# Softmax attention of a two-layer tower on one Trainium2 core: one ordered stream through the score banks

## The chip, the cores and the metric

The kernel runs on one core of one Trainium2 chip. Its engines work side by side and meet only at semaphores: TensorE (PE: matmuls and transposes, results in the eight 2 KB-a-partition banks of PSUM), VectorE (DVE), ScalarE (ACT), GpSimd (POOL) and SyncE (SP, which here issues DMAs). The metric is device time of one execution in microseconds; lower is better.

## What is computed

A tower of two layers over 16 sequences of 1024 tokens with 64 channels. Layer 0: six token embeddings, a ternary linear layer, a linear attention, a mixture of experts. Layer 1: the softmax attention that this document is about, and a second feed-forward block with attention-like parts. Between them stand residual additions and layer normalizations.

```python
h = tok(x, itok...)                       # (16, 1024, 64)
h = h + L0_attn(layernorm(h));  h = h + L0_ffn(layernorm(h))
h = h + L1_attn(layernorm(h));  h = h + L1_ffn(layernorm(h))

def L1_attn(v, WQ, WK, WV, Wout, bout):   # 8 heads of 64 channels
    q, k, val = (v @ WQ), (v @ WK), (v @ WV)          # split in heads
    scores = einsum('bshc,bthc->bsth', q, k) * SCALE
    A = softmax(scores, axis=2)
    u = einsum('bsth,bthc->bshc', A, val).reshape(B, S, H * C)
    return u @ Wout + bout
```

## The kernel before

The stages run one after the other, with a barrier between them: layer 0 (to 1019 us), `attention1` (1020 to 3472 us), statistics and residual, `feedforward1`, `finish1`. Only `attention1` is touched.

**What a head does.** The weights of a head are folded, so that the scores are x_k . (Wa x_q): `wa` makes the query of a head from the batch's input, and `wvo` folds the value and output weights. Everything wants the input transposed: `a_xh` is its float16 value and `a_xl` the rest (high and low half of a float32), both 128 partitions x 1024: two copies of the 64 channels, one in partitions 0 to 63, one in 64 to 127. A query is held likewise as `a_qh` and `a_ql`, with the 1024 queries laid as two halves of 512 over the two groups of 64 partitions. So most products run as two matmuls side by side, one on each half of the array's rows ("64*128" in the profile's rows), or, where the result has 64 rows, one on each half of its columns ("128*64").

Channel 0 of the input is set to 1. Row 0 of each half of `a_qh` is overwritten with minus the largest score of each query: the score product then gives score minus maximum, ready for the exponential. That largest score must be known before the head starts, so it is found two heads and one head ahead from a coarser product, high half times high half.

**A step.** A head has eight steps, one for each tile of 128 keys. In step kt TensorE does in this order:
1. `score(x, kt + 1)` (L1343): six matmuls of 64 x 512 into banks 0 and 1, or 2 and 3 (two score pairs in turn);
2. the side tasks of the step (table `a_tasks`): nearly always one `max` (L1298), two matmuls into two of the three banks 4, 5, 7, which VectorE reduces to a maximum per query (L1415, L1417);
3. `values(x, kt)` (L1351): exponentials times input, float32, two matmuls of 64 x 512 added into bank 6 (`A_SUM`) over the eight steps.

ScalarE takes the exponential (L1270) of a score pair to `a_prob`, four buffers. After the exponential of step 0 it copies the former head's sums from bank 6 to `a_un` (L1257), and `values(x, 0)` waits for that copy (`s.copied`).

**Other side tasks.** They too take banks of the three, in one ring numbered by j, where a task waits until the occupant three places before was taken:
- step 1, `out` (L1330): the output product of the former head, two banks; VectorE takes reciprocals of the sums of exponentials (L1429) and scales (L1431), GpSimd adds to `h` (L1221);
- step 2, `q` (L1306): the query of the head after next, one bank; ScalarE writes `a_qh` (L1249), VectorE subtracts and writes `a_ql` (L1406);
- step 6, `row` (L1321): eight transposes of one column each turn the maxima `a_mm` into rows in one bank; VectorE copies the two halves into `a_qh` (L1422, L1423);
- in head 5 of a batch, steps 3 and 5, `x` (L1314): four transposes each of the next batch's input; ScalarE writes `a_xh`, VectorE `a_xl`.

A loop (`Fori`) covers 16 heads, two batches; it runs 8 times. Each engine has the unrolled 16 heads as its own program, in the order in which the code emits it; nothing is scheduled otherwise. `feedforward1` is built differently: there ScalarE reads one ordered stream through the four score banks, its banks 4, 5, 7 hold only maxima and a row, GpSimd splits into halves, and the row goes by SyncE's DMAs. It is unchanged, and its rows are used below.

## Time and profile before

| | us |
|---|---|
| median of 3 runs (6041.11 to 6046.69) | 6045.32 |
| the profiled execution | 6043.24 |
| its span, first to last instruction | 6041.5 |
| TensorE busy (share of the span) | 5173.9 (86%) |
| VectorE busy | 4295.8 (71%) |
| ScalarE busy | 3124.6 (52%) |
| GpSimd busy | 1654.3 (27%) |
| ScalarE, exponentials of the attention (L1270), 1024 of 1113 ns | 1139.8 |
| VectorE, its maxima (L1415, L1417), 2070 of some 685 ns | 1419.0 |

The profile is that of one execution. A busy share of the span is a mean over stages with different limits; what matters for a change in one stage are the rows of that stage. A matmul's end is modelled: matmuls overlap in the array, so distances are read from start to start. A row of the timeline has start, duration, engine, line, operation, result<-operands, the part of the array (rows*columns) and the shape, and xN for N merged instructions; in brackets stands how long the engine was idle before, and whose end ended that.

### The profile page before, as it was taken

Reading aid. Unit: us, or ns where it says so; the run is one execution under the profiler, and the core shown is the slowest. Engines: PE = TensorE matmul, PEld = TensorE weight load, DVE = VectorE, ACT = ScalarE, POOL = GpSimd, SP = SyncE. Lnnn points to the kernel's source line nnn. Section 1 sums busy time; section 2 is a strip of 40 time slices with the busy share of each in tenths; the row PEclk is TensorE's granted clock in tenths of the full one; section 3 lists DMA queues with packets and bytes.
Section 4 is the critical chain, followed back from the end, with each engine's and each line's share of the span. In section 5 each row is a group of like instructions: output and inputs, shape, how many; then the busy total and the mean of one; then the engine's idle time right before and its main releaser. Section 6 shows DMA issues by size and latency. Waiting matters only on the chain. (4 is left out here: it accounts for less than half of the span.)

```text
span 6041.5 us, 124050 instructions
## 1 busy us (share of the span) xinstructions
PE 5173.9 (86%) x43090; PEld 2166.3 (36%) x43120; DVE 4295.8 (71%) x7936; ACT 3124.6 (52%) x3244; POOL 1654.3 (27%) x1572
## 2 busy tenths in 40 slices
PE   2678777999999999999999959999999999998454
PEld 1344343222222222232223224444444444443222
DVE  2666665767676767676767658888888888887666
ACT  0222221555555555555555517777777777775111
POOL 1022213000010100000000146555565565554000
PEclk9788877999999999999999959999999999998555
DMA  1211110000000000000000000000000000000000
GB/s 31 66 42 42 42 42 0 1 2 1 2 1 2 1 2 1 2 1 2 1 2 1 1 1 2 3 2 3 3 2 3 3 2 3 2 3 2 10 7 10
DMA packets 41419, 52.58 MB, mean 9 GB/s; under 512 B 31060, under 2 KB 31191, under 8 KB 40792
## 3 DMA queue, kind: packets, MB, share of 16 engines
q1 hardware_dynamic: 37734, 43.54, 2.9%
q8 instruction: 367, 6.01, 0.4%
q14 instruction: 260, 2.13, 0.1%
q10 hardware_dynamic: 3058, 0.89, 0.1%
HBM read 39.68 MB, written 4.19 MB: 7 GB/s over the span
## 5 line engine op out<-in xcount | busy, mean ns | idle before, releaser
L2054 DVE TENSOR_REDUCE f_mp<-psum 128x1 f32<-128x512 f32 (+2 forms) x2614 | 1343.5, 574 | 236.7 <-PE psum L1902 183.4
L1270 ACT ACTIVATE a_prob<-psum,escale 128x1024 f32<-128x1024 f32 x1024 | 1139.8, 1113 | 612.8 <-PE psum L1343 605.1
L1852 ACT ACTIVATE f_prob<-psum,escale_f 128x1024 f32<-128x1024 f32 x1152 | 1242.8, 1112 | 280.5 <-PE psum L1970 150.0
L1351 PE MATMUL psum<-a_prob,a_v 128*64 128x512 f32 x4096 | 1101.0, 616 | 0.1
L1415 DVE TENSOR_REDUCE a_mp<-psum 128x1 f32<-128x512 f32 x1035 | 715.5, 691 | 516.0 <-PE psum L1298 496.9
L1221 POOL TENSOR_TENSOR h<-h,a_u 128x512 f32 x129 | 163.6, 1268 | 2203.8 <-DVE a_u L1431 2203.8
L1892 PE MATMUL psum<-f_kf,f_qf 64*128 64x512 f16 (+3 forms) x3138 | 680.3, 333 | 52.0 <-DVE f_mp L2054 44.3
L1417 DVE TENSOR_REDUCE a_mp<-psum 128x1 f32<-128x512 f32 x1035 | 703.5, 680 | 0.0
L1737 POOL TENSOR_SCALAR f_hi<-f_raw,part 128x512 f16<-128x512 f32 x330 | 516.6, 1565 | 475.0 <-ACT f_raw L1819 475.0
L1983 PE MATMUL psum<-f_prob,f_vh 128*32 128x512 f32 (+3 forms) x6144 | 614.7, 495 | 3.4 <-DVE f_oc L2075 0.2
L1962 PE MATMUL psum<-f_qf,f_kf 64*128 64x512 f16 (+3 forms) x3074 | 513.7, 329 | 28.7 <-ACT f_prob L1852 12.4
L1343 PE MATMUL psum<-a_qh,a_xh 64*128 64x512 f16 x2050 | 400.8, 388 | 17.0 <-ACT a_prob L1270 14.1
L1298 PE MATMUL psum<-a_xh,a_qh 64*128 64x512 f16 x2070 | 397.7, 381 | 8.1 <-DVE a_mp L1415 7.5
L1343 PEld LDWEIGHTS psum<-a_qh,a_xh 64*128 64x128 f16 x2050 | 98.3, 93 | 850.9 <-ACT a_prob L1270 506.2
L1343 PE MATMUL psum<-a_ql,a_xh 64*128 64x512 f16 x2050 | 390.4, 377 | 0.0
L1343 PE MATMUL psum<-a_qh,a_xl 64*128 64x512 f16 x2050 | 390.2, 377 | 0.0
L1892 PEld LDWEIGHTS psum<-f_kf,f_qf 64*128 64x128 f16 x3138 | 216.9, 95 | 403.7 <-DVE f_mp L2054 353.4
L1351 PEld LDWEIGHTS psum<-a_prob,a_v 128*64 128x64 f32 x4096 | 213.2, 135 | 325.2 <-issue 238.4
L894 PE MATMUL psum<-wd,l_hT 128*128 128x512 f32 x512 | 261.5, 635 | 73.0 <-DVE l_yw L998 71.8
L1741 POOL TENSOR_TENSOR f_qf<-f_raw,f_hi 128x512 f16<-128x512 f32 x264 | 306.3, 1160 | 48.4 <-POOL f_hi L1737 48.4
L1249 ACT ACTIVATE a_qh<-psum 128x512 f16<-128x512 f32 x130 | 77.6, 597 | 453.3 <-PE psum L1306 453.3
L1899 PE MATMUL psum<-mask_q,id 64*128 64x128 bf16 x2094 | 284.4, 219 | 0.0
(396 smaller groups left out, 7434.5 us busy)
## 6 DMA issues: line engine op xcount, KB each, us to landing
l_idx<-in_itok_BS_dram SPq DMA_DIRECT2D x36, 512.0 KB, 6.4
l_idx<-in_itok_BS_dram SPq DMA_DIRECT2D x54, 256.0 KB, 7.6
l_idx<-in_x_dram SPq DMA_DIRECT2D x18, 256.0 KB, 3.7
out_dram<-h SPq DMA_DIRECT2D x16, 256.0 KB, 2.6
f_qf<-f_rowT SPq DMA_DIRECT2D x130, 4.0 KB, 1.7
wd<-in_L_ffn_Wd_dram ACTq DMA_DIRECT2D x1, 256.0 KB
wd<-in_L_ffn_Wd_dram SPq DMA_DIRECT2D x1, 256.0 KB
mgate<-in_L_ffn_gate_w_dram SPq DMA_DIRECT2D x16, 0.2 KB
```

Of the source, the lines that this page charges most:

```text
L1270: act.activation(prob[:, kt % NPB], k.psum[:, 2 * (kt % 2):2 * (kt % 2) + 2].rearrange("p b n -> p (b n)"), ACT.Exp, scale=k.escale[:]).th ...
L1298: pe.matmul(banks[r], lhsT=qh[rows_, par, t * P:(t + 1) * P], rhs=xh[rows_, bp, c * HALF:(c + 1) * HALF], start=True, stop=True).then_inc( ...
L1343: last = pe.matmul(ps[2 * (kt % 2) + r], lhsT=a[rows_, bp, keys], rhs=b[rows_, par], start=start, stop=stop)
L1351: last = pe.matmul(ps[A_SUM][half * C:(half + 1) * C], lhsT=v[:, bp, kt, 0], rhs=prob[:, kt % NPB, half * HALF:(half + 1) * HALF], start=( ...
L1415: dve.tensor_reduce(mp[:, par % 2, t, c:c + 1], banks[0], X, ALU.max).then_inc(s.taken, 1)
L1417: dve.tensor_reduce(mp[:, par % 2, t + 4, c:c + 1], banks[1], X, ALU.max).then_inc(s.taken, 1)
L1737: pool.tensor_scalar(hi[:, r % 2], raw[:, (r // 2) % 2, half], k.part[:, side:side + 1], None, ALU.mult)\
L1852: act.activation(prob[:, u % NPF], k.psum[:, pair:pair + 2], ACT.Exp, scale=k.escale_f[:])\
L1892: last = pe.matmul(bank_of(j + r)[:, col:col + nk], lhsT=qb[halves(r), qt * P:(qt + 1) * P], rhs=kb[halves(r), k0:k0 + nk], start=(y == 0) ...
L1962: last = pe.matmul(ps[pair + r][:, col:col + width], lhsT=kb[halves(r), kt * P:(kt + 1) * P], rhs=qf[halves(r), x % 4, e, q0:q0 + width], ...
L1983: last = pe.matmul(ps[F_SUM][at:at + 32, HALF - width:HALF], lhsT=vh[:, bp, 2 * n2 + r, kt], rhs=prob[:, u % NPF, r, col:col + width], sta ...
L2054: ins = dve.tensor_reduce(side[:, at:at + 1], bank_of(j + r)[:, col:col + nk], X, ALU.max)
```

## The change

Only `attention1`, its tables and two of its helper functions change. What is computed stays.

- **One stream.** The score banks, still two pairs in turn, now also carry `q`, `out` and `x`, each as one item between exponentials (`a_stream`, `A_EXTRA`): `x` after the exponential of step 0 (in head 5 only, all eight transposes at once), `q` after that of step 1, `out` after that of step 3. ScalarE reads every item in order: exponentials to `a_prob`, and the others as they are, to `a_xraw`, `a_qraw`, `a_og` (float32). TensorE makes item n + 1 when item n - 1 was read (`s.read`).
- **The three banks** hold only maxima and the row (at step 5 instead of 6); each of the two matmuls of a maximum now waits for its own bank. Four maxima instead of three run two heads ahead (`A_AHEAD`).
- **Splits on GpSimd**: cast to float16 and subtract, for input and query; GpSimd also scales the output. VectorE keeps the maxima, one reciprocal a head from SBUF (in step 6) and a copy of the row.
- **The row** is one transpose of eight columns to 8 x 128; VectorE copies it to `a_rowT`, SyncE moves it into `a_qh` with two DMAs, and the next head's first scores wait for both (`s.row_in`).
- **Values later:** `values` of tile p stands in step p + 1, so the last of a head stands in step 0 of the next; `a_prob` has eight buffers. The sums are copied after the exponential of step 1.

```diff
+A_AHEAD = 4
+A_ROW_AT = 5
+A_VALUES_AT = (1, 2, 3, 4, 5, 6, 7, 8)
+A_ORDER = ("SMV",) * T
+A_EXTRA = {0: (('x', 0),), 1: (('q', 2),), 3: (('out', -1),)}
+A_COPY_AT = 1
+A_INVERSE_AT = 6
+def a_stream(h):
+    out = []
+    for u in range(T):
+        out.append(("exp", 0, u))
+        out += [(kind, of, 0) for kind, of in A_EXTRA.get(u, ()) if kind != "x" or h == 5]
+    return out
...
++            @block.sync
+            def _(sp):
+                def row(G, par):
+                    sp.wait_ge(s.row_out, G + 1)
+                    for r in range(2):
+                        sp.dma_start(qh[r * C:r * C + 1, par].rearrange("p (t c) -> p t c", c=P),
+                                     rowT[4 * r:4 * r + 4, par % 2]).then_inc(s.row_in, 16)
...
             @block.gpsimd
+                def split_q(G, par, count):
+                    passed(pool, k.seen, s.read, count)
+                    pool.tensor_copy(qh[:, par], qraw[:, par % 2]).then_inc(s.q_hi, 1)
+                    passed(pool, k.seen, s.q_hi, G + 1)
+                    pool.tensor_tensor(ql[:, par], qraw[:, par % 2], qh[:, par], ALU.subtract).then_inc(s.q_split, 1)
...
+                    pool.tensor_tensor(u_[:], og[:, par, :, 0:C], wide(inv[:, par], C), ALU.mult).then_inc(s.scaled, 1)
+                pool.memset(prob[:, 6:8], 0.0).then_inc(s.clear, 1)
+                pool.memset(v[:, 1], 0.0).then_inc(s.clear, 1)
...
             @block.scalar
+                            act.wait_ge(s.made, SS + SR * i + n + 1)
+                            pair = 2 * ((SS + n) % 2)
+                            if kind != "exp":
+                                read_out(i, x, kind, of, pair)
+                                continue
+                            act.wait_ge(s.pv, n_pv(G - 1, part))
+                            act.activation(prob[:, part], k.psum[:, pair:pair + 2].rearrange("p b n -> p (b n)"),
+                                           ACT.Exp, scale=k.escale[:]).then_inc(s.read, 1)
+                            if part == A_COPY_AT:
+                                copy_out(G)
...
             @block.tensor
+                    for r in heads:
+                        free(i, where, j + r)
+                        pe.matmul(bank_of(j + r), lhsT=qh[halves(r), par, t * P:(t + 1) * P],
+                                  rhs=xh[halves(r), bp, c * HALF:(c + 1) * HALF], start=True, stop=True).then_inc(s.max_done, 1)
...
-                        for t in range(T):
-                            at = (t // 4) * C
-                            last = pe.transpose(banks[0][at:at + 1].bitcast(FP16)[:, (t % 4) * P:(t % 4 + 1) * P],
-                                                mm[:, t:t + 1], k.identh[:])
+                        pe.transpose(bank_of(j)[0:T].bitcast(FP16)[:, 0:P], mm[:], k.identh[:]).then_inc(s.row_done, 1)
...
+                                else:
+                                    pe.wait_ge(s.read, SS + SR * i + n)
+                                    pair = 2 * ((SS + n + 1) % 2)
+                                    if y + 1 < len(STREAMS[x]):
+                                        make(i, x, *STREAMS[x][y + 1][1:], pair)
+                                    else:
+                                        pe.wait_ge(s.row_in, 32 * (G + 2) + 64)
+                                        make(i, (x + 1) % AROUND, "exp", 0, 0, pair)
```

How the order moves, at three places. In these rows L1343 and L1449 are scores, L1298 and L1400 maxima, L1351 and L1457 values, L1330 and L1430 the output product; a name in brackets is the semaphore that the instruction waits for, and REGISTER_ALU and ISA rows work out the number to wait for.

TensorE, step 1 of a head, before: the output product stands between the maxima and the values and waits for `a1_taken`, which VectorE raises.

```order
L1288 REGISTER_ALU
L1298 MATMUL psum<-a_xh,a_qh 128x512 [waits a1_taken]
L1298 MATMUL psum<-a_xh,a_qh 128x512
L1288 REGISTER_ALU
L1330 MATMUL psum<-wvo,a_un 128x65 [waits a1_copied,a1_taken]
L1330 MATMUL psum<-wvo,a_un 128x65 x7
L1390 REGISTER_ALU
L1351 MATMUL psum<-a_prob,a_v 64x512 [waits a1_exp]
```

The same engine now, from the values in step 3 on:

```order
L1457 MATMUL psum<-a_prob,a_v 64x512 [waits a1_read]
L1457 MATMUL psum<-a_prob,a_v 64x512
L1497 REGISTER_ALU
L1430 MATMUL psum<-wvo,a_un 128x65 [waits a1_copied,a1_read]
L1430 MATMUL psum<-wvo,a_un 128x65 x7
L1386 REGISTER_ALU
L1400 MATMUL psum<-a_xh,a_qh 128x512 [waits a1_max_out]
L1386 REGISTER_ALU
L1400 MATMUL psum<-a_xh,a_qh 128x512 [waits a1_max_out]
L1457 MATMUL psum<-a_prob,a_v 64x512 [waits a1_read]
```

The output product stands ahead of the maxima, two steps later, and waits for `a1_read`, which ScalarE raises; each maximum matmul has a wait of its own.

TensorE, the row of maxima and what follows it, before (step 6):

```order
L1288 REGISTER_ALU
L1318 REGISTER_ALU [waits a1_taken]
L1321 MATMUL psum<-identh,a_mm 1x128 [waits a1_maxima]
L1321 MATMUL psum<-identh,a_mm 1x128 x7
L1288 REGISTER_ALU
L1298 MATMUL psum<-a_xh,a_qh 128x512 [waits a1_taken]
```

And now (step 5):

```order
L1386 REGISTER_ALU
L1409 REGISTER_ALU [waits a1_max_out]
L1410 MATMUL psum<-identh,a_mm 8x128 [waits a1_maxima]
L1386 ISA
L1400 MATMUL psum<-a_xh,a_qh 128x512 [waits a1_max_out]
L1386 REGISTER_ALU
L1400 MATMUL psum<-a_xh,a_qh 128x512 [waits a1_max_out]
```

Seven of eight transposes are gone; the maxima behind the row follow as before.

ScalarE from the exponential of step 0 on, before: the copy of the sums comes first, and the query is read after the exponential of step 2.

```order
L1270 ACTIVATE a_prob<-psum,escale 128x1024 [waits a1_pv,a1_scores]
L1256 REGISTER_ALU
L1257 ACTIVATE a_un<-psum 128x512 [waits a1_pv]
L1268 REGISTER_ALU
L1270 ACTIVATE a_prob<-psum,escale 128x1024 [waits a1_pv,a1_scores]
L1268 REGISTER_ALU
L1270 ACTIVATE a_prob<-psum,escale 128x1024 [waits a1_pv,a1_scores]
L1247 REGISTER_ALU
L1249 ACTIVATE a_qh<-psum 128x512 [waits a1_task]
```

And now:

```order
L1372 ACTIVATE a_prob<-psum,escale 128x1024 [waits a1_pv]
L1366 REGISTER_ALU
L1371 REGISTER_ALU [waits a1_made]
L1372 ACTIVATE a_prob<-psum,escale 128x1024 [waits a1_pv]
L1355 REGISTER_ALU
L1356 ACTIVATE a_un<-psum 128x512 [waits a1_pv]
L1366 REGISTER_ALU
L1345 REGISTER_ALU [waits a1_made]
L1346 ACTIVATE a_qraw<-psum 128x512 [waits a1_q_split]
```

The copy of the sums and the query both stand behind the exponential of step 1.

## Rows read from the trace of the kernel before

**Rows 1.** Windows: busy us (count) of PE, PEld, DVE, ACT, POOL; PE clock; DMA

```profile
1049.00:3471.00 2422.00, 2303.01 (x16018) 713.16 (x16014) 1688.41 (x3109) 1304.01 (x1320) 226.89 (x208) 1.00 0.01 1
```

**Rows 2.** Waits of TensorE, 1049 to 3471: total us, times, longest

```profile
PE psum L1330 <- DVE a_mp L1415: 99.8, 128, 0.8
```

**Rows 3.** Timeline, a plain step

```profile
2004.01 0.39 PE L1343 MATMUL psum<-a_qh,a_xh 64*128 64x512 f16 x2
...
2004.67 0.38 PE L1298 MATMUL psum<-a_xh,a_qh 64*128 64x512 f16 x2
2004.88 1.11 ACT L1270 ACTIVATE a_prob<-psum,escale 128x1024 f32<-128x1024 f32 x1 [0.86 <-PE psum L1343]
...
2004.98 1.08 PE L1351 MATMUL psum<-a_prob,a_v 128*64 128x512 f32 x4
...
2005.99 0.39 PE L1343 MATMUL psum<-a_qh,a_xh 64*128 64x512 f16 x2
```

**Rows 4.** Timeline, the step with the query product

```profile
2000.31 0.38 PE L1298 MATMUL psum<-a_xh,a_qh 64*128 64x512 f16 x2
...
2000.62 0.41 PE L1306 MATMUL psum<-a_xh,wa 128*64 128x512 f16 x2
...
2000.86 0.38 PE L1306 MATMUL psum<-a_xl,wa 128*64 128x512 f16 x2
...
2001.08 1.02 PE L1351 MATMUL psum<-a_prob,a_v 128*64 128x512 f32 x4
...
2002.04 0.39 PE L1343 MATMUL psum<-a_qh,a_xh 64*128 64x512 f16 x2
```

**Rows 5.** Timeline, the step with the output product

```profile
2015.00 0.38 PE L1298 MATMUL psum<-a_xh,a_qh 64*128 64x512 f16 x2
...
2016.16 1.11 PE L1330 MATMUL psum<-wvo,a_un 64*128 64x65 f32 x16 [0.78 <-DVE a_mp L1415]
...
2017.20 1.08 PE L1351 MATMUL psum<-a_prob,a_v 128*64 128x512 f32 x4
```

**Rows 6.** Timeline, the step with the row: first scores, maxima behind the row

```profile
2007.97 0.39 PE L1343 MATMUL psum<-a_qh,a_xh 64*128 64x512 f16 x2
...
2009.05 0.39 PE L1298 MATMUL psum<-a_xh,a_qh 64*128 64x512 f16 x2
```

**Rows 7.** Timeline, half of the next batch's input, then values

```profile
1453.81 0.66 PE L1314 MATMUL psum<-ident,a_v 128*128 128x128 f32 x4
...
1454.40 1.08 PE L1351 MATMUL psum<-a_prob,a_v 128*64 128x512 f32 x4
```

**Rows 8.** Timeline, last values of the stage and the copy of the sums

```profile
3466.72 1.08 PE L1351 MATMUL psum<-a_prob,a_v 128*64 128x512 f32 x4
...
3467.84 0.60 ACT L1257 ACTIVATE a_un<-psum 128x512 f32<-128x512 f32 x1 [2.53 <-PE psum L1351]
```

**Rows 9.** Timeline of the feed-forward's row, and landings of its DMAs (us)

```profile
3817.50 0.23 PE L1877 MATMUL psum<-identh,f_mm 128*32 128x128 f16 x1
...
3817.66 0.28 PE L1892 MATMUL psum<-f_kf,f_qf 64*128 64x256 f16 x1
...
3817.87 0.21 DVE L2063 COPY f_rowT<-psum 32x128 f16<-32x128 f16 x1 [0.37 <-PE psum L1877]
...
3818.11 1.14 SPq L1696 DMA_DIRECT2D f_qf<-f_rowT  x2
...
DMA to landing us min/median/max: 1.6/1.7/3.8
```

**Rows 10.** Feed-forward's splits by line (busy, mean ns); a memset, timeline

```profile
L1741 POOL TENSOR_TENSOR f_qf<-f_raw,f_hi 128x512 f16<-128x512 f32 x251 | 291.3, 1160 | 46.0 <-POOL f_hi L1737 46.0
...
L1726 POOL TENSOR_TENSOR f_xl<-f_xT,f_xh 128x1024 f16<-128x1024 f32 x16 | 34.2, 2135 | 2.9 <-POOL f_xh L1724 2.9
...
L1724 POOL CAST f_xh<-f_xT 128x1024 f16<-128x1024 f32 x16 | 16.6, 1038 | 0.0
...
1019.93 0.53 POOL L1224 MEMSET h<- 128x512 f32 x1 [4.78 <-SPq L1201]
```

More of the change, by code:

```diff
@@ L1140, in attention1 @@
     ps = k.bank
-    ROUND = 2 * HEADS
-    START, BEGIN, ROUNDS, TASKS = a_number()
-    assert BEGIN % 3 == 0 and TASKS % 3 == 0
+    AROUND = 2 * HEADS
+    START, ROUNDS = a_number()
+    STREAMS, first = [], 0
+    for x in range(AROUND):
+        STREAMS.append([(first + n, *item) for n, item in enumerate(a_stream(x % HEADS))])
+        first += len(STREAMS[-1])
+    SS, SR = len(A_START_STREAM), first
+    assert SR % 2 == 0
+    AT = [{(kind, part): n for n, kind, of, part in items} for items in STREAMS]
     with ExitStack() as ctx:
@@ new lines, in attention1, with previous @@
+        last_round = max(j for w, j in occupant if w == "round")
+        for d in range(3):
+            assert occupant[("start", last_start - d)][1] == occupant[("round", last_round - d)][1] == "max"
+        def previous(i, where, j):
+            j -= 3
+            if j >= 0 and (where, j) not in occupant:
+                j -= 3
+            if where == "start":
+                return emptied(0, *occupant[("start", j)]) if j >= 0 else None
+            if j >= 0:
+                return emptied(i, *occupant[("round", j)])
+            x, kind, of, part, r = occupant[("round", last_round + 1 + j)]
+            return emptied(i, x - AROUND, kind, of, part, r)
@@ new lines, in task, with make @@
+                def task(i, x, j, kind, of, part, heads, where):
+                    if kind == "max":
+                        biggest(i, x, j, of, part, heads, where)
+                    elif 0 in heads:
+                        free(i, where, j)
+                        pe.wait_ge(s.maxima, i * AROUND + x + of + 3)
+                        pe.transpose(bank_of(j)[0:T].bitcast(FP16)[:, 0:P], mm[:], k.identh[:]).then_inc(s.row_done, 1)
+                def make(i, x, kind, of, part, pair):
+                    tg = x + of
+                    banks = [ps[pair], ps[pair + 1]]
+                    if kind == "exp":
+                        last = score(x, part, banks)
@@ L1309, in task @@
[L1309 to L1323 removed]
+                                last = pe.matmul(banks[0][halves(r)], lhsT=k.wa[:, h], rhs=rhs[:, bp, r * HALF:(r + 1) * HALF],
+                                                 start=start, stop=not start, skip_group_check=True)
@@ L1336, in score @@
-                def score(x, kt, at):
+                                last = pe.matmul(banks[r][:, t * (C + 1):(t + 1) * (C + 1)], lhsT=un[halves(r), t * P:(t + 1) * P],
+                                                 rhs=k.wvo[halves(r), tg % HEADS], start=(t == 0), stop=True, skip_group_check=True)
+                    else:
+                        side = 0 if x < 0 else (x // HEADS + 1) % 2
+                        pe.wait_ge(s.prep, i * 2 + x // HEADS + 2 if x >= 0 else 1)
+                        for t in range(T):
+                            last = pe.transpose(banks[t // 4][:, (t % 4) * P:(t % 4 + 1) * P],
+                                                v[:, side, t].rearrange("p a c -> p (a c)"), k.ident[:])
@@ L1338, in score, with where_start @@
+                    last.then_inc(s.made, 1)
+                def where_start(i, x):
+                    return isinstance(i, int) and x < 0
+                def score(x, kt, banks):
                     par, bp = x % 4, (x // HEADS) % 2
@@ L1354, in values @@
+                    return last
+                def values(x, p):
+                    bp = (x // HEADS) % 2
+                    for kt in A_PARTS[p]:
+                        for half in range(2):
+                            last = pe.matmul(ps[A_SUM][halves(half)], lhsT=v[:, bp, kt, 0],
+                                             rhs=prob[:, kt, half * HALF:(half + 1) * HALF],
+                                             start=(kt == 0), stop=(kt == T - 1), skip_group_check=True)
                     last.then_inc(s.pv, 1)
@@ L1394, in _ @@
-                pe.wait_ge(s.copied, NB * HEADS + 1)
-                task(0, 0, 0, base(NB // 2), "out", -1, 0, NB * HEADS + 1)
+                last.then_inc(s.pv, NAV - sum(at >= T for at in A_VALUES_AT))
+                pe.wait_ge(s.clear, 6)
+                for n, (kind, of, part) in enumerate(A_START_STREAM):
+                    if n > 1:
+                        pe.wait_ge(s.read, n - 1)
+                    make(0, -1, kind, of + 1, part, 2 * (n % 2))
+                for j, kind, of, part in START:
+                    task(0, -1, j, kind, of + 1, part, (0, 1), "start")
@@ L1449 @@
+                inverses(1, NB * HEADS, SS + SR * (NB // 2) + 1)
 F_BANKS = (4, 5, 7)
```

410 lines of the change are left out of this document (195 added, 215 removed).

## The prediction

> **What bounds the kernel now.** I read first the busy time by stretch [rows 1]. The first attention runs from 1049 to 3471 us, 2422 us for 128 heads of one batch each, 18.92 us a head. TensorE is busy 95% of it at a granted clock of 1.00, VectorE 70%, ScalarE 54%, GpSimd 9%. So TensorE's own queue sets the time, and ScalarE, GpSimd and (less) VectorE have room. Then the waits of TensorE in that stretch [rows 2]: one alone is large, 99.8 us in 128 times, the output product (L1330) waiting for VectorE's maximum. Last, the timeline of one head, read from start to start, since the ends of matmuls are modelled and overlap the next.
>
> A plain step takes 2004.01 to 5.99, 1.98 us [rows 3]: three score pairs 0.66, the two maxima 0.31 up to the values, the values 1.01 up to the next scores. The maxima are started like a score pair, which takes 0.21-0.22, so 0.10 of the 0.31 is the change from row halves to column halves of the array; of the 1.01 about 0.15 is the change back (two products at 0.43 are 0.86). ScalarE starts the exponential 0.87 after the first score matmul and takes 1.11: it is idle for the rest of the step and nobody waits for it.
>
> What a head has beyond its eight steps (8 x 1.98 = 15.84):
> - the query product: maxima to next scores is 1.73 with it [rows 4] against 1.32 [rows 3]: **+0.41**;
> - the output product: maxima to values is 2.20 [rows 5] against 0.31: **+1.89**. Of it 1.04 is the product itself; the rest is the wait for the third bank. The timeline calls 0.78 idle, from the modelled end of the maxima; but the maxima would have let go after 0.21, so the wait is 1.16 - 0.21 = 0.95 (and 0.10 comes back, since the values behind the product pay no array change);
> - the row of maxima (eight transposes): first score to maxima is 1.08 [rows 6] against 0.66: **+0.42**.
>
> The sum is 18.56. The 0.36 up to 18.92 is the batch's input transposes and the loop's ends.
>
> **The change, part by part.**
> *Output product in the score banks.* It no longer needs two of the three maxima banks while VectorE holds them; it needs the pair of the exponential of two items before, which ScalarE has read long ago (exponential 1.11 after the scores, the pair wanted again after 1.98 or more). It keeps its 1.04. Bounds: 1.04, and 1.14 with one more array change. I take 1.04; gain 0.85.
>
> *Row of maxima.* One transpose of eight columns replaces eight. Nearest rows: in the second feed-forward one transpose of 32 columns stands for 0.16 before the next matmul [rows 9], and the change into it is about 0.10. I take +0.26 in place of +0.42 (bounds 0.16 and 0.33); gain 0.16. The way back is new: VectorE copies it to SBUF, SyncE sends two DMAs, and the next head's first scores wait for them. In the feed-forward rows the copy starts 0.37 after the transpose and takes 0.21, SyncE starts 0.03 later, its second issue 0.57 after its first, and the landing is 1.7 after the issue: 0.37 + 0.21 + 0.03 + 0.57 + 1.7 = 2.88. TensorE has meanwhile 0.16 + 0.31 + 1.01 + 0.66 + 0.31 + 1.01 = 3.46 of work. Hidden, by 0.58.
>
> *Query product.* It now comes behind values, in the same column form, and before maxima. The array changes as often as before. Bounds +0.41 and +0.51 (one more change); I take +0.44. The trace shows that a change of form costs 0.10 to 0.15 [rows 3]. The Trainium skill, TensorEngine Tiling (Array Packing), Key Properties, says that a change of tiling mode drains the engine; by that rule values and query, one mode, would follow without a gap and it would be +0.41, 4 us less in all, and the trace agrees as far as it goes (query to values has no gap, 2000.86 to 2001.08 [rows 4]).
>
> *Sums of one head end a step later.* The last values of a head now stand in step 0 of the next, and the copy of the sums must be done before the values of step 1. From the start of those last values: the copy starts at 1.12 and takes 0.60 [rows 8], then about 0.1 to TensorE: 1.82. TensorE gets there after 0.87 + 0.46 (query) + 0.11 + 0.31 = 1.75. A wait of **0.07** (bounds 0 and 0.15). ScalarE reads the exponential of step 1 before that copy; it starts at -0.09 and ends at 1.02, in time.
>
> *Head total:* 15.84 + 0.44 + 1.04 + 0.26 + 0.07 = 17.65, against 18.56: 0.91 less, x 128 = **-116 us** (bounds: 17.45, -142; 17.97, -75).
>
> *Once a batch (16 times).* Eight transposes at one place cost what 2 x 0.59 [rows 7] did. But the scores of step 1 come after them and behind the last values, so the exponential that ScalarE reads before the copy is late: scores ready at 1.01 + 0.87 = 1.88, exponential to 2.99, copy to 3.59, TensorE at 3.69, where it is ready at 1.01 + 0.66 + 0.10 + 0.46 + 0.11 + 0.31 = 2.65. With 0.1 for one more array change: 16 x 1.1 = **+17 us** (bounds 0 and 20).
>
> *Splits on GpSimd.* Rows of the feed-forward: a cast of 1024 columns 1.04, a subtraction 2.14, one of 512 columns 1.16 [rows 10]. Input 3.2, with a hand-over 3.4; query 0.5 + 1.16, with a hand-over 1.9; scaling and adding the output, two operations of 512 columns, some 2.4. A head asks 4.3 of 17.7 us. The split query is first wanted in step 4, four steps and an output product into the head: 4 x 1.98 + 1.04 + 0.66 = 9.6. The worst head is the one with the batch's input before it: read by 2.1, 2.1 + 3.4 + 1.9 = 7.4. Hidden, by 2. VectorE loses work (low halves, output, two row copies), ScalarE gains one copy of the output, about 0.6 by its copy of the sums [rows 8]; both had room.
>
> *Start and end.* Before the loop nothing covers GpSimd: the two splits, 5.3, in place of two subtractions on VectorE that I put at 0.7 each, near ScalarE's 0.60 for as many columns [rows 8]; the clearing of two more tensors (a 512 column one takes 0.53 [rows 10], these are 3072 columns: 3.2); one more pair of maxima, 1.4; that is 8.5. At the end the scaling on GpSimd costs some 1. **+9 us** (bounds 5 and 13).
>
> Sum: -116 + 17 + 9 = -90. The profiled execution took 6043.24 (span 6041.5), the median of three is 6045.32; I put the sum on the median: **5955**.
>
> **Rivals.**
> *The row lands late (slower).* Place: the first scores of each head; margin 0.58, two DMAs in a chain, and whatever is over it is paid 128 times, 12.8 us for each 0.1. For: the landings of the feed-forward reach 3.8 [rows 9], and there the row has more steps to land in. Against: the median is 1.7, the least 1.6. The gain is gone at a landing of 1.7 + 0.58 + 0.70 = 2.98, and from 3.1 on the kernel is slower. At 3.8: 1.52 x 128 = 195, 6150.
> *The change doesn't take the output product's wait away.* If the pair were not read when wanted, 0.85 x 128 = 109 would stay: 6064, slower by the start and batch terms; with half of it 6010. Against: 0.87 + 1.11 after its first score the pair is free, before it is wanted.
> *The copy of the sums gates every head.* If ScalarE reaches the copy late (say its exponential of step 1 runs 0.3 behind, as it does in the batch heads), 0.3 x 128 = 38: 5993.
> *All ends near the good bounds:* -142 + 0 + 5 is 5908; 5908 to 5930.
>
> **How the numbers follow.** Forecast 0.76, alone 5930 to 5985; the copy gating 0.08; the good end 0.07; the output wait 0.04, half of it whole and slower, half halved and faster; the late row 0.05, 0.03 of it near no change (landings of 2.9 to 3.1) and 0.02 slower. The range, 5925 to 6000, takes the first two and most of the third. What this measurement can tell from no change is 0.2%, 12 us: faster 0.76 + 0.08 + 0.07 + 0.02 = 0.93, less 0.01 for what I have not named, within 0.03, slower 0.05.
>
> **What would show it.** The wait of the output product for VectorE gone from TensorE's waits; a head at 17.6 to 17.7 from query product to query product; one transpose at the row, the next work 0.16 behind it; no wait of the first scores for the row's DMA; a wait of 1 us for the copied sums in the batch heads alone; TensorE's busy share of the stretch up from 95% to 97 or 98; nothing changed after the stage. Wrong would be: a TensorE wait on DMA once a head; a step longer than 1.98, which would say that maxima matmuls with a wait each no longer run side by side (two starts apart by 0.2 would cost 0.2 x 8 x 128 = 205); GpSimd ended later than step 4.

## The result and the profile after

The changed kernel takes 5912.99 us (median of 4, 5909.97 to 5916.78), the kernel before 6045.3: a ratio of 0.9784 [0.9772, 0.9796], 132 us less. The forecast was 5955 with a range of 5925 to 6000. The sign was right, and the wait that was to go went; the size was not: the time came out 42 us below the forecast and 12 below the range.

The windows of the stage, as in [rows 1] (busy us and count of PE, PEld, DVE, ACT, POOL; PE clock; DMA):

```profile
1054.00:3346.00 2292.00, 2261.38 (x15119) 707.21 (x15116) 1382.29 (x2433) 1354.93 (x1434) 635.07 (x626) 1.00 0.01 1
```

From the first exponential to the end it is 2292 us instead of 2422, and TensorE is busy 98.7% of it instead of 95% (97 or 98 was forecast). TensorE's waits in the middle of it (total us, times, longest), to be read beside [rows 2]:

```profile
PE psum L1457 <- ACT a_un L1356: 14.4, 16, 0.9
PE psum L1449 <- issue: 9.8, 6, 2.0
PE psum L1449 <- ACT a_prob L1372: 1.9, 1, 1.9
```

The wait for VectorE (99.8 us in 128 times) is gone. What is left are the 16 batch heads, which wait 0.9 for the copied sums, and seven loop ends. No row says that TensorE waits for the row's DMA.

The timeline of TensorE at the output product (L1430), to be read beside [rows 5]:

```profile
2006.89 1.08 PE L1457 MATMUL psum<-a_prob,a_v 128*64 128x512 f32 x4
2007.90 1.11 PE L1430 MATMUL psum<-wvo,a_un 64*128 64x65 f32 x16
2008.84 0.38 PE L1400 MATMUL psum<-a_xh,a_qh 64*128 64x512 f16 x2
2009.15 1.08 PE L1457 MATMUL psum<-a_prob,a_v 128*64 128x512 f32 x4
```

Starts are 1.01, 0.94 and 0.31 apart; a plain step has 1.01 and 0.31 there, so the product costs 0.94 and nothing is waited for. At the row of maxima, beside [rows 6], and at the query product, beside [rows 4]:

```profile
2013.55 0.22 PE L1410 MATMUL psum<-identh,a_mm 128*8 128x128 f16 x1
2013.70 0.39 PE L1400 MATMUL psum<-a_xh,a_qh 64*128 64x512 f16 x2
2014.14 1.20 SPq L1260 DMA_DIRECT2D a_qh<-a_rowT  x2
...
2019.95 1.08 PE L1457 MATMUL psum<-a_prob,a_v 128*64 128x512 f32 x4
2020.86 0.39 PE L1424 MATMUL psum<-a_xh,wa 128*64 128x512 f16 x2
2021.08 0.39 PE L1424 MATMUL psum<-a_xl,wa 128*64 128x512 f16 x2
2021.08 0.60 ACT L1356 ACTIVATE a_un<-psum 128x512 f32<-128x512 f32 x1
2021.40 0.39 PE L1400 MATMUL psum<-a_xh,a_qh 64*128 64x512 f16 x2
2021.73 1.08 PE L1457 MATMUL psum<-a_prob,a_v 128*64 128x512 f32 x4
```

The one transpose is 0.15 ahead of the maxima, the query product 0.91 behind the values. The last start of the second group is the one that the copied sums might have held: it is 0.33 behind the maxima where a plain step has 0.31. The copy itself (ACT, L1356) ends at 2021.68, just ahead of it. From one output product to the next a plain head takes 17.46 to 17.47 us; before it was 18.55 to 18.56.

The stage as a whole, from GpSimd's first clearing to ScalarE's table load behind it, went from 2452.9 us (1019.93 to 3472.85) to 2330.7 (1016.80 to 3347.47): 122.2 less. The rest of the program, whose code is the same, took 3588.6 before and 3577.6 after.

### The profile page after: what moved, and what is told of

It reads as the page before. It is cut to its first block and busy times, and to the rows that moved or that the text cites. A ratio compares the mean times of both kernels' runs of the same rounds, so it can differ in the third digit from the quotient of the medians.

```text
span 5908.2 us, 123592 instructions
## 1 busy us (share of the span) xinstructions
PE 5138.7 (87%) x42223; PEld 2156.2 (36%) x42223; DVE 3986.2 (67%) x7258; ACT 3173.6 (54%) x3356; POOL 2069.1 (35%) x1997
## 5 line engine op out<-in xcount | busy, mean ns | idle before, releaser
L1523 DVE TENSOR_REDUCE a_mp<-psum 128x1 f32<-128x512 f32 x2072 | 1333.5, 686 | 829.3 <-PE psum L1400 827.9
L1372 ACT ACTIVATE a_prob<-psum,escale 128x1024 f32<-128x1024 f32 x1024 | 1112.4, 1112 | 806.3 <-PE psum L1449 806.2
L1457 PE MATMUL psum<-a_prob,a_v 128*64 128x512 f32 x4100 | 1105.5, 618 | 14.9 <-ACT a_un L1356 14.9
L1302 POOL TENSOR_TENSOR a_u<-a_og,a_inv 128x512 f32<-128x512 f32 x129 | 134.4, 1042 | 1368.0 <-DVE a_inv L1538 1368.0
L1400 PE MATMUL psum<-a_xh,a_qh 64*128 64x512 f16 x2072 | 408.3, 382 | 3.9 <-POOL a_ql L1296 1.9
L1449 PE MATMUL psum<-a_qh,a_xh 64*128 64x512 f16 x2050 | 398.0, 384 | 11.7 <-issue 9.8
L1449 PE MATMUL psum<-a_qh,a_xl 64*128 64x512 f16 x2050 | 390.1, 376 | 0.0
L1449 PE MATMUL psum<-a_ql,a_xh 64*128 64x512 f16 x2050 | 390.1, 376 | 0.0
L1449 PEld LDWEIGHTS psum<-a_qh,a_xh 64*128 64x128 f16 x2050 | 98.8, 93 | 665.1 <-ACT a_prob L1372 210.5
L1457 PEld LDWEIGHTS psum<-a_prob,a_v 128*64 128x64 f32 x4100 | 202.7, 134 | 378.8 <-issue 331.0
L690 POOL TENSOR_TENSOR l_yw<-l_yw 128x512 f32<-128x512 f32 x64 | 81.0, 1266 | 648.9 <-DVE l_yw L998 648.9
L2067 PEld LDWEIGHTS psum<-f_qf,f_kf 64*128 64x128 f16 x3074 | 170.8, 94 | 272.2 <-issue 96.7
```

Source lines behind the costliest of these rows:

```text
L1372: act.activation(prob[:, part], k.psum[:, pair:pair + 2].rearrange("p b n -> p (b n)"), ACT.Exp, scale=k.escale[:]).then_inc(s.read, 1)
L1400: pe.matmul(bank_of(j + r), lhsT=qh[halves(r), par, t * P:(t + 1) * P], rhs=xh[halves(r), bp, c * HALF:(c + 1) * HALF], start=True, stop=T ...
L1449: last = pe.matmul(banks[r], lhsT=a[halves(r), bp, keys], rhs=b[halves(r), par], start=start, stop=stop)
L1457: last = pe.matmul(ps[A_SUM][halves(half)], lhsT=v[:, bp, kt, 0], rhs=prob[:, kt, half * HALF:(half + 1) * HALF], start=(kt == 0), stop=(k ...
L1523: dve.tensor_reduce(mp[:, tg % 2, t + 4 * r, c:c + 1], bank_of(j + r), X, ALU.max)\
L2067: last = pe.matmul(ps[pair + r][:, col:col + width], lhsT=kb[halves(r), kt * P:(kt + 1) * P], rhs=qf[halves(r), x % 4, e, q0:q0 + width], ...
```

## The experiments

All times are medians beside the kernel before on the same chip. Unless said otherwise the edit is made in the changed kernel.

**Is it the wait alone?** An edit of the kernel before: the output product behind the values of its step, the query product a step later. Banks and engines stay as they were.

```
-    slots[2].append(("q", 2, 0))
+    slots[3].append(("q", 2, 0))
...
                             values(x, kt)
+                            for item in late:        # the output product
+                                task(*item)
```

> The kernel before with two edits in its order alone: in step 1 TensorE does the output product behind the values instead of ahead of them, and the query product stands in step 3 instead of 2. Same banks, same engines, same products. Theory A (what the change gained is the output product's wait for the third maxima bank, 0.95 us a head, and nothing else of size): VectorE now reads the maxima during the 1.01 us of the values, so the wait goes without any new bank or engine; VectorE needs 1.1 us for the output's two banks and the scores of the next step cover 0.66 of it and the maxima's first matmul more. The head falls from 18.56 to 17.61-17.75, the time to 5925-5945. Theory B (the three banks are too few wherever the product stands, and the gain needed the product in the score banks): the wait moves to the maxima of step 2, 0.7 us or more, and the time stays at 6015 or above.

5981.1, ratio 0.9891 [0.9874, 0.9907]: 64 us less than the kernel before, between the two theories. A head takes 18.01. The timeline:

```profile
2014.75 1.11 PE L1330 MATMUL psum<-wvo,a_un 64*128 64x65 f32 x16
2015.70 0.38 PE L1343 MATMUL psum<-a_qh,a_xh 64*128 64x512 f16 x2
2015.91 0.38 PE L1343 MATMUL psum<-a_qh,a_xl 64*128 64x512 f16 x2
2016.13 0.38 PE L1343 MATMUL psum<-a_ql,a_xh 64*128 64x512 f16 x2
2016.75 0.39 PE L1298 MATMUL psum<-a_xh,a_qh 64*128 64x512 f16 x2 [0.24 <-DVE a_u L1437]
```

The product has its 0.95, and the next maxima come 1.05 behind the first scores instead of 0.66: a wait of 0.40 for VectorE's scaling of the product, where there had been 0.95. So this order alone gives about half of the gain. Of the other half 0.40 a head is the wait that the ring of three banks still makes here, and some 0.17 is the row of maxima, which this run leaves at eight transposes. Whether another order in the same three banks would lose that wait too, no run shows.

**What does the output product cost by itself?** It stands behind the maxima of step 3 and ahead of its values.

```
-A_ORDER = ("SMV",) * T
+A_ORDER = ("SMV",) * 3 + ("MSV",) + ("SMV",) * 4
```

> The changed kernel with the output product behind the maxima of step 3 and ahead of its values, instead of between the values of step 2 and the maxima; nothing else moves. It asks what the output product's own time is: 1.04 up to the next start was the prediction, 0.94 was measured before the maxima, 0.95 before scores. Theory A (0.94 is the product, 16 matmuls, and there is 0.10 of array change in it wherever fp16 work in row halves and column halves meet, so an order with as many changes costs the same): 5913 within 3. Theory B (in row halves the product's tail runs beside the maxima, also in row halves, and behind it the values must wait for the array): 1.04 to the values instead of 0.94, +0.10 to +0.15 a head, 5926-5932.

5903.5, ratio 0.9766 [0.9751, 0.9781]: faster by 9 than the changed kernel, which neither theory had. The intervals of the two ratios overlap, but the heads tell them apart: 17.37 here, 17.46 there. The rows say why:

```profile
2000.93 0.39 PE L1400 MATMUL psum<-a_xh,a_qh 64*128 64x512 f16 x2
2001.15 1.00 PE L1430 MATMUL psum<-wvo,a_un 64*128 64x65 f32 x16
2002.08 1.08 PE L1457 MATMUL psum<-a_prob,a_v 128*64 128x512 f32 x4
2003.10 0.39 PE L1449 MATMUL psum<-a_qh,a_xh 64*128 64x512 f16 x2
```

Behind maxima, which are in row halves as it is, the product starts after 0.22 like any follower in the same form, and the values come 0.93 later. Maxima to values is 1.15 with it and 0.31 without: 0.84. So it costs 0.94 where it stands in the changed kernel and 0.84 here.

The number of changes of form is the same in both orders: row halves are entered once behind values and left once ahead of values. The difference lies in the product. It is 16 matmuls, and a timeline that begins inside it shows the start of its last two and what follows. In the kernel before, the changed kernel and this run:

```profile
2016.99 0.28 PE L1330 MATMUL psum<-wvo,a_un 64*128 64x65 f32 x2
2017.20 0.65 PE L1351 MATMUL psum<-a_prob,a_v 128*64 128x512 f32 x2
```
```profile
2008.73 0.28 PE L1430 MATMUL psum<-wvo,a_un 64*128 64x65 f32 x2
2008.84 0.38 PE L1400 MATMUL psum<-a_xh,a_qh 64*128 64x512 f16 x2
```
```profile
2001.88 0.28 PE L1430 MATMUL psum<-wvo,a_un 64*128 64x65 f32 x2
2002.08 0.65 PE L1457 MATMUL psum<-a_prob,a_v 128*64 128x512 f32 x2
```

From the product's first start to these last two is 0.83 behind a wait (2016.16), 0.83 behind values (2007.90) and 0.73 behind maxima (2001.15). From there to the next start is 0.11 where maxima follow and 0.20 to 0.21 where values do. So the 1.04 in [rows 5] is 0.83 + 0.21: 0.10 of it is the change into column halves, and another 0.10 belongs to a product that begins behind a wait or a change of form.

**The row of maxima.** The transpose is done eight times over.

```
-                        pe.transpose(bank_of(j)[0:T].bitcast(FP16)[:, 0:P], mm[:], k.identh[:]).then_inc(s.row_done, 1)
+                        for n in range(8):
+                            last = pe.transpose(bank_of(j)[0:T].bitcast(FP16)[:, 0:P], mm[:], k.identh[:])
+                        last.then_inc(s.row_done, 1)
```

> The changed kernel with the one transpose of the row of maxima (eight columns) done eight times over into the same bank. Theory A (each transpose costs its own 0.02-0.03, as 0.42 for eight before and 0.25 for one now say): 0.16-0.21 a head more, 5933-5940. Theory B (the 0.25 is nearly all change of form and a transpose alone costs the 0.053 that 0.42 / 8 gives): 7 x 0.053 = 0.37, 5960. If the number of transposes does not matter at all: 5913.

5967.7, ratio 0.9871 [0.9854, 0.9887], 55 more than the changed kernel. A head takes 17.85, 0.385 more, or 0.055 for each of seven transposes: theory B.

```profile
2016.56 0.61 PE L1411 MATMUL psum<-identh,a_mm 128*8 128x128 f16 x8
2017.10 0.39 PE L1400 MATMUL psum<-a_xh,a_qh 64*128 64x512 f16 x2
```

0.54 from first transpose to maxima against 0.15 with one, so of the 0.26 that the row costs some 0.06 is the transpose; the rest goes with the changes of form around it (0.31 from the last scores to the transpose, where scores follow scores after 0.22). The eight transposes of the kernel before had one column each and took 0.33 to the maxima (2009.05 in [rows 6]), so they were cheaper apiece than eight of eight columns:

```profile
2008.72 0.40 PE L1321 MATMUL psum<-identh,a_mm 128*1 128x128 f16 x8
```

**The copied sums.** ScalarE copies them twice, first into a tensor that nobody reads.

```
+                    act.activation(un2[:], ps[A_SUM], ACT.Copy)
                     act.activation(un[:], ps[A_SUM], ACT.Copy).then_inc(s.copied, 1)
```

> The changed kernel with ScalarE copying the sums twice, the first time into a tensor that nobody reads, so that the copy that TensorE waits for ends 0.60 later in each head. Theory A (in regular heads the copy ends at 2021.68 and the values start at 2021.73, so there is no slack left and the missing wait of 0.07 was a matter of hundredths): the whole 0.60 shows less the slack of 0.05, 0.55 x 128 = 70 us, 5983. Theory B (the hand-over has slack that the trace does not show, 0.2 or more): 5960 or less.

5981.1, ratio 0.9892 [0.9875, 0.9908]. The waits, and the two copies in the timeline of a plain head:

```profile
PE psum L1459 <- ACT a_un L1358: 67.5, 123, 1.4
```
```profile
2052.11 0.60 ACT L1357 ACTIVATE a_un<-psum 128x512 f32<-128x512 f32 x1
2052.60 0.59 ACT L1358 ACTIVATE a_un<-psum 128x512 f32<-128x512 f32 x1
```

The second copy starts 0.49 behind the first (0.47 to 0.48 in the batch heads), so that is the delay put in, not the 0.60 that I wrote. A head takes 17.95, 0.485 more. All of the delay is paid: there is no slack to be seen at this place. That is theory A with a smaller delay; 0.485 x 128 is 62 us, and the median is 64 to 68 above the two of the changed kernel.

**The place of the batch's input.** First step 5, then step 2, instead of step 0:

```
-A_EXTRA = {0: (('x', 0),), 1: (('q', 2),), 3: (('out', -1),)}
+A_EXTRA = {1: (('q', 2),), 3: (('out', -1),), 5: (('x', 0),)}
...
+A_EXTRA = {1: (('q', 2),), 2: (('x', 0),), 3: (('out', -1),)}
```

> The changed kernel with the batch's eight input transposes behind step 5's scores instead of step 0's, in the same heads. Theory A (in 16 batch heads TensorE waits 0.90 for the copied sums only because the input's reading on ScalarE, 1.02, and a whole item stand ahead of the copy): the wait goes, the batch head falls from 2.21 to 1.3 over a plain one, 16 x 0.90 = 14 us less, 5899. Theory B (the item costs the same wherever it stands, since ScalarE's 1.02 then delays another exponential that TensorE waits for): 5911-5915.

5959.5, ratio 0.9855 [0.9838, 0.9871]: 47 us slower than the changed kernel, which neither theory had. TensorE's waits in the middle of the stage and the timeline where one arises:

```profile
PE psum L1424 <- POOL a_xl L1289: 40.1, 15, 2.7
```
```profile
2041.27 1.04 POOL L1302 TENSOR_TENSOR a_u<-a_og,a_inv 128x512 f32<-128x512 f32 x1 [11.87 <-DVE a_inv L1538]
2042.50 1.26 POOL L1305 TENSOR_TENSOR h<-h,a_u 128x512 f32 x1 [0.19 <-POOL a_u L1302]
2043.71 1.04 POOL L1287 CAST a_xh<-a_xraw 128x1024 f16<-128x1024 f32 x1
2044.93 2.12 POOL L1289 TENSOR_TENSOR a_xl<-a_xraw,a_xh 128x1024 f16<-128x1024 f32 x1 [0.18 <-POOL a_xh L1287]
...
2047.19 0.41 PE L1424 MATMUL psum<-a_xh,wa 128*64 128x512 f16 x2 [2.67 <-POOL a_xl L1289]
```

The wait for the copied sums is gone (one of 0.5 is left), as expected, but the input's split now stands in GpSimd's queue behind the scaling of the output, which waits (11.87 idle) for VectorE's reciprocal in step 6. The next batch's query product then waits 2.67. And TensorE's granted clock falls with it. The windows behind this wait, and at the wait 148 us earlier:

```profile
2047.00:2051.00 4.00, 3.81 (x16) 0.91 (x18) 1.29 (x2) 0.60 (x1) 1.81 (x3) 0.65 0.00 0
2051.00:2055.00 4.00, 4.00 (x34) 1.75 (x32) 1.59 (x3) 2.62 (x3) 0.00 (x0) 0.92 0.01 4
1898.10:1904.80 6.70, 6.04 (x24) 1.51 (x24) 1.29 (x2) 1.61 (x2) 2.28 (x3) 0.50 0.01 2
```

It fell at 12 of the stage's 16 such waits (the row above counts 15 of them, up to 3300). A batch head with the wait and no fall took 21.22; with the clock down for 3.4 us, as at the first two windows, 22.8 to 22.9; and five of them, where it was down for 6.8 us, as at the last, 24.0 to 24.1.

> The changed kernel with the batch's input transposes in step 2 (an item behind step 2's exponential) instead of step 0, the place where they stood in step 5 having cost 46 us because GpSimd split the input behind the output's scaling, which waits for VectorE until step 6. Theory A (GpSimd's queue was all that was wrong with step 5): in step 2 the split stands ahead of the output's scaling, the query product of the next batch does not wait, the wait for the copied sums (0.90, 16 times) is gone too, the batch head falls from 19.67 to 18.8, the time by 14 us to 5899. Theory B (ScalarE's 1.02 for the input makes something late wherever it stands): 5911 or more.

5896.0, ratio 0.9749 [0.9734, 0.9764]: 17 less than the changed kernel, theory A. In step 2 the split is ahead of the scaling, and no wait for `a_xl` is left. One wait of 0.5 for the copied sums is left in the stretch, and a batch head takes 18.61, 1.15 over a plain one instead of 2.2.

**The start.** Beside the input in step 2, the two new clearings go behind the preparation of the first batch, and TensorE waits for them later, ahead of the loop's first scores.

```
+                prepare_batch(0, 0, 0)
                 pool.memset(prob[:, 6:8], 0.0).then_inc(s.clear, 1)
                 pool.memset(v[:, 1], 0.0).then_inc(s.clear, 1)
...
-                prepare_batch(0, 0, 0)
```

> The input transposes in step 2, and at the start of the stage GpSimd clears the two tensors (1.80 and 0.95) behind the preparation of the first batch, where it waits for ScalarE 3.32, instead of ahead of it. Theory A (the 8 us that the start became longer are GpSimd's queue, in sequence): 2.7 less at the start beside the 14 of the batches, 5896. Theory B (the start is set by something else, such as the maxima or the row): 5899, as with the input in step 2 alone.

5888.1, ratio 0.9746 [0.9733, 0.976]. The intervals of this run and the last overlap, but their traces tell them apart: from the first clearing to the first exponential 34.7 (1013.46 to 1048.17) where the changed kernel has 37.4 (1016.80 to 1054.19) and the one before 29.4, and the whole stage is 2310.8 against 2313.6. That is theory A's 2.7; the medians are 8 apart, and in the two traces what is over 2.8 lies outside the stage.

**The row's DMA.** The row of maxima is transposed in step 6 instead of 5.

```
-A_ROW_AT = 5
+A_ROW_AT = 6
```

> The changed kernel with the row of maxima transposed one step later (step 6 instead of 5), which takes 1.98 us of TensorE's work from above its way through VectorE and two DMAs. It measures the margin that the prediction put at 0.58 and the price of the late row. Theory A (way of 2.88 from the transpose to the landing, as worked out from the feed-forward's rows; cover then 3.45 - 1.98 = 1.47): TensorE waits 1.4 a head for the row's DMA, 1.4 x 128 = 180, 6093, slower than the kernel before. Theory B (the small DMA lands sooner, say 1.0 after its issue): 0.7 x 128 = 90, 6003. If the row had no DMA on the path at all: 5913.

6107.8, ratio 1.0104 [1.0089, 1.012]: slower than the kernel before.

```profile
PE psum L1449 <- DMA a_qh<-a_rowT: 162.5, 121, 2.2
```

A head takes 18.84 to 18.87, so 1.38 to 1.40 of waiting, and the margin that the changed kernel has is 1.98 - 1.39 = 0.59; the prediction had 0.58. 1.39 x 128 is 178, within 2 us of theory A's 180 and its 6093; the 15 us above that go with nine falls of the granted clock in this run and with one longer wait an iteration, up to 2.2. The rival was real, and it stood where it was put.

**The values one step late.** The values of a key tile go back to its own step and the copy of the sums to step 0, as before; the ordered stream stays.

```
-A_VALUES_AT = (1, 2, 3, 4, 5, 6, 7, 8)
+A_VALUES_AT = (0, 1, 2, 3, 4, 5, 6, 7)
...
-A_COPY_AT = 1
+A_COPY_AT = 0
```

> The changed kernel with the one-step lag of the values undone: the values of a key tile stand in its own step (as in the kernel before) and the sums are copied behind the exponential of step 0. It asks two things. First, whether the lag itself gives or takes anything in a head: the values of step 0 must then wait for the copied sums, whose copy starts behind the exponential of step 0 as before, so I expect 17.46 a head either way. Second, the loop's end, where TensorE was idle 2.1-2.8 before and is idle 1.4-2.0 after. Theory A (the lag makes the difference, because the last work ahead of the loop's branch, the values, no longer waits for the exponential just made): idle of 2.1 or more again, with falls of the granted clock behind some of them, an iteration 287-288.5 instead of 286.0, the time 5920-5930. Theory B (it comes from something else in the loop): 1.4-2.0, 286, the time 5909-5917.

6034.8, ratio 0.9984 [0.9975, 0.9993]. Nearly the whole gain is gone: a head takes 18.44. The copy goes back too, since the values of step 0 wait for it. The waits of TensorE and a place where one arises:

```profile
PE psum L1457 <- ACT a_prob L1372: 111.8, 264, 0.4
```
```profile
2003.00 2.12 ACT L1372 ACTIVATE a_prob<-psum,escale 128x1024 f32<-128x1024 f32 x2 [1.49 <-PE psum L1449]
2003.36 0.38 PE L1400 MATMUL psum<-a_xh,a_qh 64*128 64x512 f16 x2
2004.16 1.08 PE L1457 MATMUL psum<-a_prob,a_v 128*64 128x512 f32 x4 [0.42 <-ACT a_prob L1372]
```

Where a query or output product is an item of the stream, two pairs of scores follow each other with no values between, and the values of the second pair's step reach TensorE before its exponential is done: 0.80 behind the maxima instead of 0.31, twice a head, 0.98 in all. The lag is what makes room for the extra items of the stream. I had asked the run about something else, and had expected 17.46.

**The loop's end.** GpSimd holds TensorE at the head of the loop with one more subtraction, behind its last work of the iteration (its setting up is left out here).

```
+                    pool.wait_ge(s.pv, n_pv(G, 6))
+                    pool.tensor_tensor(idle_b[:, 0:HALF], idle_a[:, 0:HALF], idle_a[:, 0:HALF], ALU.subtract).then_inc(s.idle, 1)
...
                 with pe.Fori(0, NB // 2) as i:
+                    pe.wait_ge(s.idle, i + 1)
```

> The changed kernel with TensorE held at the start of each loop iteration until GpSimd has done one more subtraction of 512 columns (1.16), queued behind its last work of the iteration. TensorE's idle at the loop's end grows from 1.41 to about 2.6, near the 2.52 of the kernel before; nothing else is changed. Theory A (the granted clock falls after such an idle, as in four of six iterations of the kernel before and after the 2.67 waits of the run with the input in step 5): an iteration takes 1.2 for the idle and 1.2 to 2 for the clock more, 286.0 to 288.5-289.2, the time 5930-5936. Theory B (the idle costs itself alone): 287.2 an iteration, 5922.

5921.4, ratio 0.9792 [0.9779, 0.9806], near theory B. TensorE's idle became 2.35 in all seven loop ends; the granted clock fell behind the first of them alone (0.57 in the four us behind it) and stayed at 1.00 behind the six others. An iteration took 286.7, 0.7 more than in the changed kernel, and the one with the fall 288.3. So an idle as long as those of the kernel before did not bring as many falls: there they came behind four of seven.

**Together:** input in step 2, clearings behind the preparation, output product behind the maxima.

> All three edits together: input transposes in step 2, the two clearings behind the first batch's preparation, the output product behind the maxima of step 3. Theory A (they are independent: 17, 25 together at most with what the run to run spread leaves, and 9.5): 5876-5882. Theory B (the output product behind the maxima collides with the input item in step 2, since both now stand within one step on ScalarE): 5888 or more.

5882.7 (5876.2 to 5887.0), ratio 0.973 [0.9717, 0.9743]; a plain head 17.37, a batch head 18.50, an iteration 282.3. It is the fastest here, some 30 us below the changed kernel, and at the edge of what was expected of it; its stage is 2298.3.

**Both kernels again**, unchanged.

> The kernel before once more, unchanged, for its profile: the parts of the program outside the first attention, whose code is the same in both kernels, took 11 us less in the one profile of the changed kernel than in the one of the kernel before. Theory A (spread between executions; among the runs so far these parts took 3573 to 3590): anywhere in 3575-3590 again, no difference that stays. Theory B (something of the change reaches into them): 3588 or more here, and 3580 or less in the changed kernel run again.

> The changed kernel once more, unchanged, for its profile, as the pair of the kernel before run again. Theory A: the parts outside the first attention anywhere in 3575-3590. Theory B: 3580 or less.

6043.6, ratio 1.0001 [0.9991, 1.001], and 5916.8, ratio 0.9787 [0.9774, 0.9801]. The stage repeats to 0.6 us: 2452.3 and 2330.4. The rest of the program was 3581.2 in the kernel before and 3577.4 in the changed one. It was 3581 to 3590 in three profiles with the old stage and 3574 to 3587 in twelve with the new, 6 less on the mean with a spread of 4 to 5 between profiles of either kind. So both lie in theory A's range; whether a few of the 11 us are the change's, these runs can't say.

## Why the prediction was wrong in size

The forecast was -90. The stage gave -122, and that number is firm (twice to 0.6 us). The 32 in it that I missed, step by step, from values to values as in the rows above:

- **Plain step**, 1.98: right, in all runs. Of its 1.01 from values to scores I had put 0.15 down to the change of form; it is 0.10, since the query product in the same form follows the values after 0.91.
- **Output product: the step that failed.** I took it at 1.04, as [rows 5] have it behind maxima and a wait, and wrote that the values behind it "pay no array change". They do: the 1.04 holds 0.10 of it, as the last starts above show. In the new place maxima follow, and the change stands between them and the values, in the 0.31 of the plain step, so my sum had it twice. Measured: 2.26 from values to values with the product between them, and 2.63 where two pairs of scores now follow each other, less two plain steps (3.96): 0.93. That is 0.11 x 128 = 14 us, and its whole gain is 0.96 a head, the wait of 0.95, where I had 0.85. My bounds for the term were 1.04 and 1.14, so they did not hold it; with 0.93 in the sum the same width of range would have begun at 5911.
- **Query product and copied sums**: forecast 0.44 and a wait of 0.07. Measured 1.78 + 2.63 - 3.96 = 0.45 for both, of which 0.02 is the wait (0.33 against 0.31): 0.07 x 128, 8 us less. The doubled copy shows that the place is as tight as I had it, with no slack; what was off was a few hundredths in the sum of the way.
- **Row** +0.26, as forecast (2.24 from values to values).
- Together a head is 17.465 instead of 17.65: 0.185 x 128 = 24 us. My good bound for the head was 17.45, so it did hold this, but by luck: it was made of 0.16 for the row, which took 0.26, and 1.04 for the product, which took 0.93.
- **Batch**, +1.1: measured 1.04 (19.67 less 17.46, against 19.73 less 18.56), and for the reason given, a wait of 0.90 for the copy. **Start**, forecast 8.5: measured 8.0. **End**, forecast 1: measured 1.2, from the last exponential to the end of the stage.
- **Loop ends**: not in my sum, which put them at nothing without a reason. From output product to output product an iteration took 302.6 on average before and 286.05 after. Less its heads that is 302.6 - 16 x 18.555 - 2 x 1.17 = 3.4 before and 286.05 - 16 x 17.465 - 2 x 2.21 = 2.2 after, so 1.2 in each of seven, 9 us. Two rows of before and one of after:

```profile
1650.06 1.08 PE L1351 MATMUL psum<-a_prob,a_v 128*64 128x512 f32 x4
1653.66 0.39 PE L1343 MATMUL psum<-a_qh,a_xh 64*128 64x512 f16 x2 [2.52 <-ACT a_prob L1270]
```
```profile
1625.85 0.39 PE L1449 MATMUL psum<-a_qh,a_xh 64*128 64x512 f16 x2 [1.41 <-issue]
```

The idle itself is 2.1 to 2.8 before and 1.4 to 2.0 after. The larger part is what follows it. In the kernel before the clock fell behind four of seven loop ends, as behind the one above, and an iteration with such a fall took 303.4 on average against 301.6 without, so the falls make 1.8 x 4/7 = 1.0 of the 1.2:

```profile
1653.00:1657.00 4.00, 3.34 (x16) 0.80 (x18) 1.29 (x2) 1.29 (x2) 0.00 (x0) 0.72 0.03 6
1657.00:1661.00 4.00, 3.22 (x28) 1.31 (x22) 1.87 (x5) 1.11 (x1) 0.00 (x0) 0.85 0.00 0
1654.90:1658.10 3.20, 3.20 (x12) 0.43 (x8) 1.11 (x2) 0.92 (x2) 0.00 (x0) 0.50 0.00 0
```

In the changed kernel it fell behind none of fourteen (two profiles). Why its loop end is shorter and has no falls is not settled: with the lag undone the mean idle was 2.00, between 1.67 in the changed kernel and 2.40 in the one before, with falls behind three of seven. So the lag gives 0.33 of the 0.73, and what gives the rest stays open.

- The sum of these: 24 and 9, against the 32 that the stage came out lower.
- The rest of the 42 us, some 10, lies in the parts whose code is the same, and is within their spread.

Of the rivals, the late row was real and 0.59 away. The rival by which all ends near the good bounds (5908 to 5930) came true in its number, with chance 0.07, but not by its terms: the row, the batch and the start were as forecast, not at their good ends, and the product's term, the loop ends and the rest of the program made up for them.

One more thing the prediction didn't see, though no number hung on it. It took the values' lag as a cost (0.07) with nothing on the other side. It is a condition of the gain with this stream: without it 0.98 a head is lost again, and the change was worth 10 us.

## What to carry to other kernels

A start-to-start distance read from a trace belongs to what stands before and behind it, and to whether the engine had waited. When a step is moved, read its cost from rows with the new neighbours, count each change of form once, and let the bound reach to the cheapest pair. Before an operation is put into a queue, look at what stands in each engine's queue ahead of it: the same input took 64 us more in step 5 than in step 2 (5959.5 against 5896.0), for one reciprocal on another engine and the falls of the clock that the wait brought. Count the loop's ends apart from what repeats inside.

## What the runs showed of the hardware

- A stream of matmuls in row halves is followed 0.31 later by one in column halves, and 0.22 later by one in row halves; values are followed after 1.01 by row halves and after 0.91 by column halves. So a change costs about 0.10 each way. The Trainium skill, TensorEngine Tiling (Array Packing), Key Properties, has a change of tiling mode drain the engine, and the rows agree as far as the gap goes (0.31 at a change, 0.22 without). What it costs still hangs on the order: the output product behind maxima instead of values, with as many changes, saved 0.09 a head, because its 16 matmuls took 0.73 instead of 0.83 from the first start to that of the last two.
- TensorE's granted clock fell from its upper level (2.4 GHz, 1.00) to its lower one (1.2 GHz, 0.50) at some idle times inside the busy loop, and did not at others of the same length: at 12 of 16 of 2.67, one of seven of 2.35, and at no loop end with up to 1.83 of idle in any profile here; the shortest with a fall was 1.86. It stayed down for 3.4 us, and for 6.8 at five of those of 2.67. The shorter cost 1.6 (22.87 against 21.22, 288.3 against 286.7), the longer 2.8 (24.07 against 21.22).
- Two copies of 512 columns on ScalarE, 0.60 each by the record, start 0.47 to 0.49 apart.
